# Routing of two token groups at once in a gated attention and mixture-of-experts block

## What is computed

```python
x = x + tanh(g_xattn[0]) * xattn(layernorm(x), ctx, mask, Wq, Wkv)
x = x + tanh(g_ffn[0]) * ffn(layernorm(x), w_router, fc1_w, fc2_w, gate_w, up_w, down_w)

# ffn
logits = x @ w_router
top_logits, top_idx = top_k(logits, 2)
scores = softmax(top_logits)
sorted_idx = argsort(top_idx.reshape(-1))
# each expert: silu(proj) * gate @ fc2_w[e] over the rows sorted to it
moe_out = (unperm.reshape(-1, 2, H) * scores[:, :, None]).sum(axis=1)
shared = silu(x @ gate_w) * (x @ up_w) @ down_w
return moe_out + shared
```

## Time and profile before

| what | value |
|---|---|
| device time, median of 3 runs | 360.67 us (360.33 to 360.98) |
| profiled execution | 361.57 us |
| its span, first to last instruction | 359.5 us |
| TensorE matmul busy | 312.0 us (87%) |
| VectorE busy | 255.8 us (71%), 780 instructions |
| ScalarE busy | 170.8 us (48%) |
| GpSimd busy | 121.2 us (34%) |

### The profile page before, as it was taken

One profiled execution on the slowest core, in us unless ns is written; L12 is line 12 of the kernel. 1 busy time (PEld: TensorE's weight loads), 2 busy tenths in 40 slices (PEclk: granted clock), 3 DMA queues, 4 the chain that ended last, 5 costly groups with the idle time before them and its releaser, 6 DMA issues.

```text
span 359.5 us, 7932 instructions
## 1 busy us (share of the span) xinstructions
PE 312.0 (87%) x2404; PEld 253.1 (70%) x2404; DVE 255.8 (71%) x780; ACT 170.8 (48%) x325; POOL 121.2 (34%) x133
## 2 busy tenths in 40 slices
PE   1948879888888895775996999999999999999994
PEld 1836767677767684654443758898888888988884
DVE  5367569698989898883799763767676767644786
ACT  2344757665757464544566051644444444433231
POOL 4541111216161616055162016383434343432000
PEclk9998999999999987888898999999999999999999
DMA  8676585866475546211025200233333232211683
GB/s 229 212 207 195 156 236 146 206 181 189 148 200 165 166 138 188 92 62 59 2 74 162 60 2 16 73 97 99 103 98 99 90 104 90 86 42 27 264 289 121
DMA packets 34916, 46.50 MB, mean 129 GB/s; under 512 B 5599, under 2 KB 29539, under 8 KB 34370
## 3 DMA queue, kind: packets, MB, share of 16 engines
q1 hardware_dynamic: 28002, 28.77, 28.6%
q10 hardware_dynamic: 3424, 8.72, 7.7%
q0 software_dynamic: 3456, 8.56, 7.1%
HBM read 21.55 MB, written 12.62 MB: 95 GB/s over the span
## 4 chain that ended last, share of the span: by engine, by line
PE 57%; SPq 12%; DVE 10%; DMA 8%; issue 4%; ACT 4%; another core or an unknown queue 2%; POOL 1%; ACTq 1%; DVEq 0%; POOLq 0%
PE ps L1589 31%; SPq L352 7%; DMA stacks<-work 6%; SPq L359 4%; PE ps L1275 3%; PE ps L1476 2%; DVE mx L893 2%; PE ps L1639 2%; PE ps L1561 2%; PE ps L1340 2%; PE ps L1373 2%; PE ps L1389 2%; PE ps L1581 2%; ACT probs L623 2%
## 5 line engine op out<-in xcount | busy, mean ns | idle before, releaser
L541 POOL DMA_INDIRECT expert_rows<-v_s,slot_u x39 | 38.4, 984 | 61.9 <-ACT v_s L806 49.2
L893 DVE TENSOR_REDUCE mx<-ps 128x8 f32<-128x1024 f32 x32 | 39.1, 1223 | 12.5 <-PE ps L1340 11.8
L503 POOL TENSOR_TENSOR work<-work 128x512 bf16<-128x512 f32 x16 | 18.6, 1162 | 66.0 <-ACT work L592 66.0
L623 ACT ACTIVATE probs<-ps 128x1024 f32<-128x1024 f32 x32 | 32.6, 1019 | 15.5 <-PE ps L1373 8.5
L1193 DVE TENSOR_TENSOR act<-ps,sil 128x256 f32<-128x256 f32 x39 | 16.6, 425 | 29.9 <-ACT sil L799 21.7
L1589 PE MATMUL ps<-fc_hi,xs_hi 128*128 x78 | 34.2, 438 | 0.0
L799 ACT ACTIVATE sil<-ps 128x256 f32<-128x256 f32 x39 | 15.0, 385 | 39.3 <-PE ps L1589 38.2
L1340 PE MATMUL ps<-stacks 96*128 96x128 bf16 x256 | 21.3, 230 | 12.5 <-DVE mx L893 6.4
L1589 PE MATMUL ps<-fc_lo,xs_hi 128*128 x78 | 30.9, 396 | 0.0
L1589 PE MATMUL ps<-fc_hi,xs_lo 128*128 x78 | 30.8, 394 | 0.0
L1340 PEld LDWEIGHTS ps<-stacks 96*128 96x128 bf16 x256 | 16.9, 104 | 17.3 <-DVE mx L893 8.9
(11 more groups left out here) (207 smaller groups left out, 818.3 us busy)
## 6 DMA issues: line engine op xcount, KB each, us to landing
stacks<-work SPq DMA_DIRECT2D x93, 128.0 KB, 2.7
xs_in<-dispatched SPq DMA_DIRECT2D x39, 129.0 KB
fc_s<-in_fc ACTq DMA_DIRECT2D x8, 512.0 KB, 3.6
stacks<-expert_rows SPq DMA_DIRECT2D x4, 1024.0 KB, 6.0
fc_s<-in_fc ACTq DMA_DIRECT2D x8, 256.0 KB, 4.0
ctx_s<-in_ctx_t SPq DMA_DIRECT2D x8, 192.0 KB
x_all<-in_x SPq DMA_DIRECT2D x1, 1536.0 KB, 8.9
out<-x_all SPq DMA_DIRECT2D x3, 512.0 KB, 6.2
```

What stands on the lines that cost most here:

```text
L503: nc.gpsimd.tensor_tensor(out[:, 2, :], rest, out[:, 1, :], ALU.subtract).then_inc(ready, 1)
L541: nc.gpsimd.indirect_dma_start(ys, bass.IndirectOffsetOnAxis(dst_u[:, r:r + 1], 0), y_out[:, r, :], None, bounds_check=2 * T - 1, oob_is_e ...
L623: nc.scalar.activation(probs[:, 2 * j + h], ps_t, ACT.Exp, scale=HD ** -0.5).then_inc(probs_ok[j][h], 1)
L893: nc.vector.reduce_max(mx[:, j, 8 * h:8 * h + 8], ps_s, AX_X).then_inc(max_ok[j][h], 1)
```

## The change

Groups 0 to 5 are routed as three pairs (0, 1), (2, 3), (4, 5), groups 6 and 7 alone: five units. `logits` still runs for each group; `choice`, `chosen`, the Exp of two scores, `positions`, `places` and `weights` run once for a unit, in the stage of its last group, over four tiles where there were two. The running sums `cum` hold one state and not two: TensorE adds the counts of the earlier tiles of a unit itself (14 small matmuls for a pair, 4 for a single group), and `places` adds the counts of the unit with a new reduce and one add. The wait for `cum_ok` moves from VectorE to TensorE. The second pair's rows lie in the place of `hid_0`; therefore the first `gate_tanh` waits for the scatters of groups 2 and 3. The wait of `norm2` and `weights` for earlier scatters stays for groups 4 and 5 in `norm2` alone. `slot_u` has a place for each group. `dispatch` runs one stage later in the loop, and in the tail GpSimd has `dispatch` of groups 4, 5, 6 and 7, with `power2(7, 0)` behind the first indirect DMA of group 4 and `power2(7, 1)` before the last of group 5. Left out below: sizes of tiles, the totals that SyncE and ScalarE wait for, and `choice`, `second_score` and the middle of `weights`, which change only as `chosen` does.

```diff
-        rows_of = [row_s[:, g % 2] for g in range(G - 2)] + [row_6[:, :, :], row_7[:, :, :]]
+        row_h = nc.alloc_sbuf_tensor_at("row_h", [P, 2, 4, ROW], F32, offset=start["hid_0"])
+        rows_of = ([row_s[:, 0], row_s[:, 1], row_h[:, 0], row_h[:, 1], row_s[:, 0], row_s[:, 1]]
+                   + [row_6[:, :, :], row_7[:, :, :]])
+        units = [(0, 1), (2, 3), (4, 5), (6,), (7,)]
+        ended = {unit[-1]: u for u, unit in enumerate(units)}
+        rows_in_unit = [home[:, :, :, :].rearrange("p g m c -> p (g m) c") for home in (row_s, row_h, row_s)
+                        ] + [row_6[:, :, :], row_7[:, :, :]]
+        ALL_0, ALL_1 = 64 * (G - 2), 64 * 2 + 16
...
             def dispatch(g):
-                pool.wait_ge(slots_ok, g + 1)
-                pool.wait_ge(w_ok, g + 1)
-                pool.wait_ge(dup_ok[0], g + 1)
-                pool.wait_ge(dup_ok[1], g + 1)
+                u = g // 2 if g < 6 else g - 3
+                if g == units[u][0]:
+                    pool.wait_ge(slots_ok, u + 1)
+                    pool.wait_ge(w_ok, u + 1)
+                    pool.wait_ge(dup_ok[0], units[u][-1] + 1)
+                    pool.wait_ge(dup_ok[1], units[u][-1] + 1)
                 for m in range(4):
+                    if (g, m) == (G - 4, 1):
+                        power2(G - 1, 0)
+                    if (g, m) == (G - 3, 3):
+                        power2(G - 1, 1)
                     nc.gpsimd.indirect_dma_start(
-                        xs, bass.IndirectOffsetOnAxis(slot_u[:, g % 2, m:m + 1], 0), rows_of[g][:, m, :], None,
-                        bounds_check=NULL_ROW + P - 1, oob_is_err=False).then_inc(scat[g % 2], 16)
+                        xs, bass.IndirectOffsetOnAxis(slot_u[:, g, m:m + 1], 0), rows_of[g][:, m, :], None,
+                        bounds_check=NULL_ROW + P - 1, oob_is_err=False).then_inc(scat[u == 1], 16)
...
             for s in range(2, G + 2):
                 if live(s - 3):
                     power2(s - 3, 0)
-                if live(s - 5):
-                    dispatch(s - 5)
+                if live(s - 6):
+                    dispatch(s - 6)
                 if live(s - 3):
                     power2(s - 3, 1)
                 if live(s):
                     third(s, kst, k_rest, k_ok[1], k_pc, k_ok[2])
                     third(s, qst, q_rest, q_ok[1], q_pc, q_ok[2])
 
+            dispatch(G - 4)
             dispatch(G - 3)
-            power2(G - 1, 0)
-            power2(G - 1, 1)
             dispatch(G - 2)
             dispatch(G - 1)
...
                 sa.wait_ge(gu0_done, j + 1)
+                if j == 0:
+                    sa.wait_ge(scat[1], ALL_1)
                 if j >= 2:
...
-                elif 1 <= g < G - 2:
-                    ve.wait_ge(scat[g % 2], 64 * (g // 2) + 16 * (g % 2))
+                elif 4 <= g < G - 2:
+                    ve.wait_ge(scat[0], 64 * 2)
...
             def chosen(g):
 
-                nc.vector.max_index(topi[:, 0, :], top[:, 0, :], lg[:, 0, :]).then_inc(dve_link, 1)
-                links[0] += 1
-                link(nc.vector.max_index(topi[:, 1, :], top[:, 1, :], lg[:, 1, :]))
-                link(nc.vector.tensor_copy(idx_f[:, :].rearrange("p (j k) -> p j k", j=2), topi[:, :, 0:2]))
-
-                link(nc.vector.tensor_tensor(oh[:, :, :, :].rearrange("p j k e -> p (j k) e"),
-                                             e_f[:, :].unsqueeze(1).broadcast_to([P, 4, 8]),
-                                             idx_f[:, :].unsqueeze(2).broadcast_to([P, 4, 8]), ALU.is_equal))
-                ve.wait_ge(cum_ok, g + 1)
-                link(nc.vector.tensor_tensor(cnt[:, :, :], oh[:, :, 0, :], oh[:, :, 1, :], ALU.add))
-                nc.vector.tensor_tensor(cum[:, 1, :], cum[:, 0, :], cnt[:, 0, :], ALU.add).then_inc(oh_ok, 1)
+                if g not in ended:
+                    return
+                n = 2 * len(units[ended[g]])
+                for j in range(n):
+                    nc.vector.max_index(topi[:, j, :], top[:, j, :], lg[:, j, :]).then_inc(dve_link, 1)
+                links[0] += n
+                ve.wait_ge(dve_link, links[0])
+                link(nc.vector.tensor_copy(idx_f[:, 0:2 * n].rearrange("p (j k) -> p j k", k=2), topi[:, 0:n, 0:2]))
+
+                link(nc.vector.tensor_tensor(oh[:, 0:n, :, :].rearrange("p j k e -> p (j k) e"),
+                                             e_f[:, :].unsqueeze(1).broadcast_to([P, 2 * n, 8]),
+                                             idx_f[:, 0:2 * n].unsqueeze(2).broadcast_to([P, 2 * n, 8]), ALU.is_equal))
+                nc.vector.tensor_tensor(cnt[:, 0:n, :], oh[:, 0:n, 0, :], oh[:, 0:n, 1, :], ALU.add).then_inc(oh_ok, 1)
 
             def places(g):
 
-                ve.wait_ge(pos_done, g + 1)
-                nc.vector.tensor_tensor(slot[:, :, :], ps_c[:, 192:208].rearrange("p (j e) -> p j e", j=2),
-                                        er_f[:, :].unsqueeze(1).broadcast_to([P, 2, 8]), ALU.add
+                if g not in ended:
+                    return
+                u, n = ended[g], 2 * len(units[ended[g]])
+                ve.wait_ge(pos_done, u + 1)
+                nc.vector.tensor_tensor(slot[:, 0:n, :], ps_c[:, 192:192 + 8 * n].rearrange("p (j e) -> p j e", j=n),
+                                        er_f[:, :].unsqueeze(1).broadcast_to([P, n, 8]), ALU.add
                                         ).then_inc(pos_read, 1)
-                ve.wait_ge(pos_read, g + 1)
-                link(nc.vector.tensor_tensor(slot_p[:, :, :, :], oh[:, :, :, :],
-                                             slot[:, :, :].unsqueeze(2).broadcast_to([P, 2, 2, 8]), ALU.mult))
-                link(nc.vector.reduce_sum(slot_f[:, :], slot_p[:, :, :, :].rearrange("p j k e -> p (j k) e"), AX_X))
-                if g >= 1:
-                    ve.wait_ge(scat[g % 2], 64 * (g // 2) + 16 * (g % 2))
-                nc.vector.tensor_copy(slot_u[:, g % 2, :], slot_f[:, :]).then_inc(slots_ok, 1)
-                nc.vector.tensor_tensor(cum[:, 0, :], cum[:, 1, :], cnt[:, 1, :], ALU.add).then_inc(cum_ok, 1)
+                ve.wait_ge(pos_read, u + 1)
+                link(nc.vector.tensor_tensor(slot_p[:, 0:n, :, :], oh[:, 0:n, :, :],
+                                             slot[:, 0:n, :].unsqueeze(2).broadcast_to([P, n, 2, 8]), ALU.mult))
+                link(nc.vector.reduce_sum(slot_f[:, 0:2 * n],
+                                          slot_p[:, 0:n, :, :].rearrange("p j k e -> p (j k) e"), AX_X))
+                nc.vector.tensor_copy(slot_u[:, units[u][0]:g + 1, :].rearrange("p g m -> p (g m)"), slot_f[:, 0:2 * n]
+                                      ).then_inc(slots_ok, 1)
+                if g < G - 1:
+                    link(nc.vector.reduce_sum(new[:, :], cnt[:, 0:n, :].rearrange("p j e -> p e j"), AX_X))
+                    nc.vector.tensor_tensor(cum[:, :], cum[:, :], new[:, :], ALU.add).then_inc(cum_ok, 1)
 
             def weights(g):
 
-                ve.wait_ge(ex_ok, g + 1)
...
-                link(nc.vector.tensor_copy(rows_of[g][:, :, D], dest_f[:, :]))
-                nc.vector.tensor_scalar(dest_f[:, :], dest_f[:, :], -4.0, None, ALU.add).then_inc(w_ok, 1)
-                ve.wait_ge(w_ok, g + 1)
+                half = 4 * (u == len(units) - 1)
+                nc.vector.tensor_copy(rows_in_unit[u][:, :, D], dest_f[:, half:half + 2 * n]).then_inc(w_ok, 1)
+                ve.wait_ge(w_ok, u + 1)
+                if n == 4:
+                    link(nc.vector.tensor_scalar(dest_f[:, :], dest_f[:, :], -8.0, None, ALU.add))
...
                 if g:
-                    pe.wait_ge(pos_read, g)
+                    pe.wait_ge(lg_read, g)
+                if g >= 2:
+                    pe.wait_ge(pos_read, g // 2 if g < G - 1 else len(units) - 1)
...
             def positions(g):
 
-                pe.wait_ge(oh_ok, g + 1)
+                if g not in ended:
+                    return
+                u, n = ended[g], 2 * len(units[ended[g]])
+                pe.wait_ge(oh_ok, u + 1)
+                pe.wait_ge(cum_ok, u + 1)
                 pe.wait_ge(maxt_ok[1], min(g + 3, G))
-                for j in range(2):
-
-                    nc.tensor.matmul(ps_c[:, 192 + 8 * j:200 + 8 * j], before[:, :], cnt[:, j, :],
-                                     start=True, stop=False)
-                    last = nc.tensor.matmul(ps_c[:, 192 + 8 * j:200 + 8 * j], ones_b[:, :], cum[:, j, :],
-                                            start=False, stop=True)
+                for j in range(n):
+
+                    at = ps_c[:, 192 + 8 * j:200 + 8 * j]
+                    nc.tensor.matmul(at, before[:, :], cnt[:, j, :], start=True, stop=False)
+                    for i in range(j):
+                        nc.tensor.matmul(at, ones_b[:, :], cnt[:, i, :], start=False, stop=False)
+                    last = nc.tensor.matmul(at, ones_b[:, :], cum[:, :], start=False, stop=True)
```

(6 more changed lines are left out.)

94 lines of the change are left out of this document (53 added, 41 removed).

## The result

The changed kernel takes **356.24 us** (median of 17 runs, 353.79 to 362.38). The kernel before, run beside it, takes 359.15 (17 runs, 355.87 to 361.51). The ratio is 0.9922, 95% interval 0.9894 to 0.9951, so 2.9 us less, where the forecast had 1.5 less. The miss has two parts of nearly one size. The forecast was put on the median of the first three runs, 360.67, and with 17 runs the same kernel has 359.15, 1.5 us lower. The other 1.4 us is gain that the forecast didn't have. Two later repeats, in other sets of runs, gave 0.9988 (0.9920 to 1.0056) and 0.9923 (0.9865 to 0.9981); the kernel before against itself gave 0.9953 (0.9901 to 1.0004). So with six to a dozen runs half a per cent can't be told here, and the 17 carry the verdict.

What follows compares the result with a forecast made beforehand. Bound before 160 us: stages from mx through norms, transposes and SyncE's transfers to the next scores; from 195, TensorE. Terms -1.0 - 0.4 + 0.3 - 0.4 = -1.5 us took 360.67 to 359.1, own range 358.5 to 359.8, with rivals 357.4 to 362.6.

Steps and rivals of the forecast that it cites:

- The step that failed: In the stages, choice, one-hot and weights were taken to run in VectorE's idle time, so shrinking them was priced at nothing.
- The stages: Four stages by their mx: near 72 -0.4 us, 89 -0.4, 107 -0.6, 125 +0.3, from places removed or widened.
- From mx to the transposes: Stretch from score reduce to normed tokens' transposes: 2.8 to 3.0 us near 72 and 107, about 3.1 near 89.
- The Exp near 89: ScalarE's Exp no longer waits 1.66 us, since group 0's run of indirect DMAs moves a stage later.
- Positions at 0: TensorE's ten more small matmuls per pair cost between 0 and 1.7 us; taken as 0.
- The tail: From 160 to 195 us: fewer VectorE operations and waits, second power's delay within slack, unnamed wait unchanged; -0.4 us.
- Rival B: Tail: unnamed wait before ot_s goes, ot_s some 3 us earlier, second power caps the gain at 0.9: 358.2 us; chance 0.11.
- Rival C: Tail: the longer run of indirect DMAs holds TensorE's reports, ot_s starts at 173.8: 363.3 us, slower; chance 0.16.
- Rival D: Near 155 us: group 3's run holds the report of group 7's maxima transpose, about 1 us stays: 360.1; chance 0.12.
- Rival E: Stages gain nothing, since the Exp or the shared port holds the transposes as before: about 360.6 us; chance 0.16.

Runs made afterwards that it cites:

- e11: Kernel before plus eight small VectorE copies behind the choice in each of five stages: 370.81 us, 1.0338 of the kernel before.
- e2: Changed kernel with group 7's second power moved ahead of group 5's first indirect DMA: 358.22 us, 0.9923 of the kernel before.
- e8: Changed kernel, group 7's second power ahead of group 5's run, GpSimd waiting for the last group's places before group 6's run: 349.06 us, 0.9698 of before.
- e13: Same kernel as e2, in other runs, changed kernel with the second power early and no pause: 351.09 us, 0.9783 of the kernel before.
- e16: Same kernel as e8, on the chip of other runs: 351.43 us, 0.9759 of the kernel before.
- e3: Kernel before with both powers of group 7 ahead of group 5's run of indirect DMAs: 362.51 us, 1.0024 of the kernel before.
- e18: Kernel before, unchanged, run and profiled again: 357.46 us, 0.9953 of itself.
- e4: Kernel before with the two norms right behind the first operation of places, the rest of places after them: 363.50 us, 1.0050 of the kernel before.
- e1: Changed kernel, unaltered, run and profiled again: 361.40 us, 0.9988 of the kernel before.
- e15: Changed kernel, unaltered, on the chip of other runs: 357.40 us, 0.9923 of the kernel before.

## Why the prediction was right or wrong

**The step that failed** is the sentence "Choice, one-hot and weights lie behind mx reduces that end well before the DMA; their time goes into idle time." VectorE has hardly any such idle time: in the stage from 89.51 to 107.32 it is busy 16.06 us of 17.81 in some fifty instructions with hand-overs between them, and stands only 0.81 us ahead of the next mx. I had read the chain of waits, which names one path (SyncE's ten microseconds of issues), and took all that isn't on it for slack. e11 measured that slack: adding 9.0 us of copies there cost 10.7. Because of this step the sum priced only the four to six instructions between mx and the transposes and gave nothing for the others of the 52 that went.

**The stages, forecast -1.1 us** (-0.4, -0.4, -0.6, +0.3). The two profiles of before have 69.7 us on the mean for four stages, the three of the changed kernel 66.1: -3.6. VectorE's busy time fell from 62.8 to 56.6, by 6.2, and its wait for scores ahead of mx rose from 3.2 to 6.0. These means mix executions with held reports and without. Like with like, with the four kernels whose loop is the changed kernel's (e2, e8, e13, e16) and e3 for the loop of before: with held reports 72.3 and 68.8 us, -3.5, for 6.7 less of VectorE; without, 67.8 (e18 alone) and 65.7, -2.1, for 5.2 less. One to five executions stand behind each of these means. So 40 to 53% of what was taken from VectorE shortened the stages, two to three times the forecast, and the rest became a wait for TensorE's scores, the next bound (TensorE is busy 15.04 of the 15.31 us from 78.67), which the forecast didn't price because it had no gain to be given back. The clock is no rival for this: the gain lies in the first three stages, 52.6 to 49.0 us on the mean of the two and the three profiles, in all of which it is 1.00 but for one with 0.96.

**From mx to the transposes.** Forecast 2.8 to 3.0 us near 72 and 107 and 3.1 near 89; in the first profile after, 2.84 and 2.25, and 3.80 near 89. The first holds. The second is shorter than told. In the last slot_u was to give 0.75, and it is indeed 0.17 now, but the wider slot_p, an instruction earlier, takes 0.93 there instead. The forecast's sum for it was in any case one execution's: e18 has 2.76 near 89 without the change. e4 speaks against its setting the stage.
The two rows that change places are 0.93 at slot_u and 0.93 at slot_p. The Trainium skill, SBUF — State Buffer, section "SBUF: two separate sides", says of the port pair that VectorE and GpSimd share: whichever of a VectorE operation (in a two-port mode, or with two inputs from SBUF against a GpSimd operation that reads SBUF) and one of GpSimd starts first holds it for the whole instruction, and the other is blocked. The trace agrees: slot_p, with two inputs from SBUF, starts at 95.33 inside GpSimd's subtraction (95.02 to 96.18) and ends at 96.26; at 128.97, behind a subtraction that ended at 128.71, it takes 0.23.
The gain that I took from slot_u belonged to one execution's timing (2.19 us of slot_u in four stages in one profile of before, 0.68 in the other).

**The Exp near 89** no longer waits: it starts at 93.40, 0.21 us behind what it waits for (forecast: not waiting 1.66). Right, but no test of the reason: e18 doesn't wait there either. In e1, which has held reports, the Exp near 89 isn't held and the one at 106.34, behind the first run, is, by 1.58 us; that fits the reason.

**VectorE's instructions:** 52 fewer, forecast some 50.

**Positions at 0:** nothing in the runs speaks against it; TensorE's busy time in a stage is as before. (A single group has 5 small matmuls in the trace, from 175.38 on, not the 4 of the section on the change.)

**The tail, forecast -0.4.** From group 6's transposes to down_0 it takes 34.7 us on the mean of three profiles where the two of before have 33.5: +1.2. The power stood behind the seventh indirect DMA just as told (172.11, 173.10, norm at 173.72 for a forecast of 173.5), and its lateness was within slack as told: the slots came at 175.71. What failed is that nothing was put down for TensorE behind them. With ot_s early it had done its first gate products by 170.60, stood idle for 4.78 us, and took 2.82 us for the next four at a granted clock of 0.59. Before, it idled 4.13 us ahead of 169.26, and the low clock (0.50 from 169.26 to 173.58) fell on the first gate products, ahead of the counts: these were ready at 174.64, TensorE took them up at 175.64, and from there on its clock was 1.00. The prediction named a clock that falls in other stretches as what would upset it; here it cost the tail about 1 us. Taking the power out of the run is worth 5 to 6 us of the tail (e13).

**Do the parts add up?** Not in the profiles. The four stages give -3.6, the fifth stretch (from the mx near 144 to the transposes of group 6: 17.4 before, 17.9 after) +0.5, the tail +1.2: -1.9, where the timing has -2.9. The stretch ahead of the mx near 72 gives +3.3, over half of it from the one execution with 78.67; of the routing it holds only group 0's norms and, before, its choice, and it varies from 71.5 to 78.7 us over all profiles of both kinds of loop. So the gain of 2.9 us stands on the timing, and the profiles show where VectorE's time went and which way each part moved.

**Rival B** happened in part: ot_s at 165.86 was its sign ("before 166"), and in e1, with held reports, it waits 1.58 us only. Its price was right in its cap, that the power and the norm hold what follows. That it would gain 0.9 is not seen; the clock took that back. And the 4.68 us that it starts from are of an execution with held reports; the second profile of before has 2.47 with a named cause.
**Rival C** (a run holds TensorE's reports until it ends; slower) has a mechanism that the 18 rows above show in some executions, but what it forecast for ot_s didn't happen in any profile of the changed kernel: ot_s started at 165.86, 0.3 us after the second indirect DMA did (165.54), with seven of the tail's eight done only at 173.08.
**Rival D** happened in two executions. In the first profile of the changed kernel the maxima's transpose at 155.72 was copied at 155.99, within a run of indirect DMAs, and in e15 likewise. In e1 and in e2, which has the same loop, it was copied 2.7 us after the transpose began, where D's sign is "more than 1 us", and the stretch around it takes 19.41 and 18.75 us where the profiles of before's loop with held reports have 18.0 to 18.2: the "about 1 us" that D names.
**Rival E** (the stages gain nothing) was wrong by the stage lengths.

**The base.** 360.67 was the median of three runs within 0.7 us of each other, and the kernel's runs spread over 5.6 us (355.87 to 361.51). The range carried the unknown costs of the change but nothing for the base, and that alone moves it by 1.5. With the base of 359.15 the forecast would have been 357.7, and the measured 356.24 inside a range that began at 355.9. The 0.7 us that the prediction took as what a measurement can tell is small as well: the interval of these 17 runs is 1.0 us to either side.
